# The last chunk of a fused Mamba and expert layer: tiles of 4 states by 256 tokens, and a back half per 256 tokens

## The reference

```python
x = x + attn(layernorm(x))           # attn: y of the scan below, then residual + out inside
x = x + ffn(layernorm(x))            # 8 experts, each for 512 tokens in a row
# attn(x): xn = rmsnorm(x, rms_w); xs, res = split(xn @ W_in)       (512 + 512 channels)
xs = silu(causal_conv4(xs) + conv_b)
dt, Bm, Cm = split(xs @ W_x, [512, 528]); dt = softplus(dt @ W_dt)
A = -exp(A_log)                                                     # 512 channels x 16 states
h = exp(A * dt_t) * h + dt_t * B_t * xs_t                           # per token, channel, state
y_t = sum over states of h * C_t
out = residual + (y * silu(res)) @ W_out
# ffn(x), per expert e: silu(x @ w1[e]) * (x @ w3[e]) @ w2[e]       (256 -> 704 -> 256)
```

## Time and profile before

| what | us |
|---|---|
| median of three runs | 988.26 |
| profiled execution, span of its core | 989.0 |
| PE, DVE, ACT, POOL busy in that span | 922.8, 900.1, 731.6, 891.3 |
| 512 scans, L657 | 623.5 |
| 255 products by C on POOL, L515 | 598.8 |
| 109 and 145 BU products, POOL L501 and DVE L642 | 257.9 and 173.1 |
| 512 exps, L786 | 347.0 |

### The profile page before, as it was taken

The page is one execution under the profiler, slowest core; times in us unless marked ns, Lnnn a source line. Parts: engine busy times, 40 slices in busy tenths (PEclk is TensorE's granted clock), DMA queues, the critical chain, the costliest instruction groups (busy, mean ns, idle before and its releaser), DMA issues.

```text
span 989.0 us, 13017 instructions
## 1 busy us (share of the span) xinstructions
PE 922.8 (93%) x4172; PEld 601.7 (61%) x4172; DVE 900.1 (91%) x966; ACT 731.6 (74%) x1305; POOL 891.3 (90%) x424
## 2 busy tenths in 40 slices
PE   6998998999999999999999999999999998769898
PEld 4555455655866566755756557655767556755765
DVE  5789899899999999999999999999999989999951
ACT  4566877888779877888788887888788786567530
POOL 0388899999999999999999999999999999999920
PEclk9898999999999999999999999999999999679899
DMA  5490136011651038111571037210580127200110
GB/s 174 173 343 22 43 134 252 1 67 59 247 209 45 23 115 351 49 67 43 195 276 43 25 102 299 114 67 0 187 327 3 44 75 290 107 22 1 61 50 21
DMA packets 43476, 116.82 MB, mean 118 GB/s; under 512 B 8592, under 2 KB 27024, under 8 KB 34192
## 3 DMA queue, kind: packets, MB, share of 16 engines
q1 hardware_dynamic: 41552, 115.94, 31.5%
q10 hardware_dynamic: 1856, 0.04, 0.1%
HBM read 110.21 MB, written 5.77 MB: 117 GB/s over the span
## 4 chain that ended last, share of the span: by engine, by line
PE 37%; DVE 36%; ACT 15%; issue 11%; DMA 1%; DVEq 0%; SPq 0%; ACTq 0%
DVE ring L657 25%; PE gbank L1090 19%; DVE ring L642 9%; PE ybank L1153 7%; PE gbank L1104 7%; ACT ebank L786 4%; ACT hb L1019 2%; ACT sres L867 1%; ACT xs L863 1%; PE gbank L1098 1%; ACT L1015 1%; ACT L875 1%; ACT L871 1%; DMA hb<-in_L_attn_W_x_dram 1%; PE gbank L1224 1%
## 5 line engine op out<-in xcount | busy, mean ns | idle before, releaser
L657 DVE TENSOR_TENSOR_SCAN ring<-ebank,state,ring 128x512 f32<-128x512 f32 x512 | 623.5, 1266 | 32.7 <-ACT ebank L786 25.7
L515 POOL TENSOR_TENSOR hc<-ring,c_all 128x1024 f32<-128x1024 f32 x255 | 598.8, 2364 | 17.4 <-DVE ring L657 9.6
L786 ACT ACTIVATE ebank<-dt_,a_neg 128x512 f32<-128x512 f32 x512 | 347.0, 689 | 163.2 <-DVE ring L657 160.6
L1153 PEld LDWEIGHTS ybank<-ident,hc 128*128 128x128 f32 x2048 | 240.2, 145 | 102.9 <-issue 53.1
L1153 PE MATMUL ybank<-ident,hc 128*128 128x128 f32 x2048 | 267.7, 280 | 28.3 <-POOL hc L515 19.6
L501 POOL TENSOR_TENSOR ring<-b_all,u 128x1024 f32<-128x1024 f32 x109 | 257.9, 2366 | 10.5 <-DVE taken L606 9.5
L642 DVE TENSOR_TENSOR ring<-b_all,ubank 128x1024 f32<-128x1024 f32 x145 | 173.1, 1194 | 0.0
L1090 PE MATMUL gbank<-xT,w 128*128 128x512 f32 x320 | 148.9, 599 | 14.7 <-DVE hb L737 11.9
L1090 PE MATMUL gbank<-xT,w_a 128*128 128x512 f32 x256 | 120.2, 606 | 8.0 <-DVE dt_ L631 4.4
L1090 PEld LDWEIGHTS gbank<-xT,w 128*128 128x128 f32 x320 | 57.7, 191 | 82.1 <-issue 57.1
L1090 PE MATMUL gbank<-xs,w_a 128*128 128x512 f32 x224 | 100.8, 593 | 0.7 <-ACT sres L804 0.7
(11 more groups left out here) (145 smaller groups left out, 777.1 us busy)
## 6 DMA issues: line engine op xcount, KB each, us to landing
b_all<-bc_kept SPq DMA_DIRECT2D x32, 1024.0 KB, 6.6
c_all<-bc_kept SPq DMA_DIRECT2D x32, 1024.0 KB, 8.4
w<-in_L_ffn_w_dram SPq DMA_DIRECT2D x16, 640.0 KB, 4.8
w_a<-in_L_attn_W_in_dram SPq DMA_DIRECT2D x7, 1024.0 KB, 4.9
w_a<-wc_kept SPq DMA_DIRECT2D x7, 1024.0 KB, 4.8
w2s<-in_L_ffn_w_dram SPq DMA_DIRECT2D x8, 640.0 KB, 9.3
xin<-in_L_attn_x_dram SPq DMA_DIRECT2D x9, 512.0 KB, 3.5
x<-in_L_attn_x_dram SPq DMA_DIRECT2D x7, 512.0 KB, 6.4
```

What stands on the lines that cost most here:

```text
L515: ch_ok.by(e.tensor_tensor(hc[:, q % HC, :, :], ring[:, q % RING, :, :], c_all[:, n:n + NG, :], ALU.mult))
L657: h_ok.by(e.tensor_tensor_scan(row, ebank[j % 2][:, :], row, initial=state[:, q, n:n + 1], op0=ALU.mult, op1=ALU.add))
L786: e_ok.by(e.activation(ebank[j % 2][:, :], dt_[:, d, :], ACT.Exp, scale=a_neg[:, d, k:k + 1]))
L1153: last = e.matmul(ybank[:, cols(b)], hc[:, q % HC, n, cols(b)], ident[:, :], is_transpose=True, start=(k == 0 and n == 0 and b == 0), stop ...
```

## The change

In chunk 7 the tiles of blocks d = 2 and 3 hold SN = 4 states of HF = 256 tokens. Tiles 16 to 23 are the first 256 tokens (d 2 in 16 to 19, d 3 in 20 to 23), tiles 24 to 31 the second 256. So there are 64 scans and 64 exps of 256 for 32 and 32 of 512. The number of tiles, of products by C and of their elements stays. POOL has 15 BU tiles in this chunk for 14. `u_half` copies both blocks' u for one half of the tokens to ubank. PE's lag is 2 tiles from tile 24 on.

The back half of chunk 6 has its own table in iteration 7, `FINAL`, most of it some four tiles earlier (SiLU after tile 16 for 20, contractions at 20 and 21 for 24 and 28). The first 256 tokens of chunk 7 then go through gating, projection, statistics, normalising, turning, and gate and up products of 256 columns (two results to a bank, "GT" and "UH") beside tiles 22 to 31; SiLU, products and the contractions of blocks 0 and 1 follow after the last exp. The second 256 tokens go through the same after the last scan, with the contractions of blocks 0 and 1 between their steps. The dummy matmuls are gone. Tables for iterations 0 to 6 are the same. The diff, cut:

```diff
+    POOL_BU_E = (1, 4, 7, 8, 11, 14, 16, 17, 18, 19, 21, 23, 25, 26, 29)
+    QH = Q // 2
+    HF = TC // 2
+    SN = 2 * NG
+    LAG_E = 2
+    SWITCH = 24
...
+        FINAL = [
+            (3, "back", "YT", 3, 4.4), (4, "back", "M", 0, 8.9), (4, "back", "M", 1, 8.7), (10, "back", "OXT", 0, 10.9),
+            (11, "back", "GATE", 0, 13.2), (12, "scan", "YT", 0, 12.9), (12, "back", "GATE", 1, 13.4), (13, "back", "GATE", 2, 14.2),
+            (13, "back", "GATE", 3, 14.4), (14, "back", "GATE", 4, 15.2), (14, "back", "TAIL", 0, 16.9), (14, "back", "UP", 0, 16.3),
+            (16, "back", "UP", 1, 16.5), (17, "back", "UP", 2, 17.3), (17, "back", "UP", 3, 18.3), (18, "back", "UP", 4, 19.3),
+            (19, "back", "DOWN", 0, 22.9), (20, "scan", "YT", 1, 20.8), (20, "back", "DOWN", 1, 23.9), (21, "ahead", "M", 0, 28.9),
+            (23, "ahead", "YH", 0, 24.2), (25, "ahead", "YH", 1, 26.2), (26, "ahead", "M", 1, 40.0), (27, "ahead", "OXH", 0, 28.6),
+            (28, "ahead", "GT", 0, 29.5), (28, "ahead", "GT", 1, 29.7), (29, "ahead", "GT", 2, 30.7), (30, "ahead", "UH", 0, 31.5),
+            (30, "ahead", "YH", 2, 31.2), (31, "ahead", "UH", 1, 34.0)]
         LAST = [
...
+            (0, "back", "UH", 2, 3.2), (2, "back", "YH", 3, 2.9), (4, "back", "DN", 0, 9.0), (6, "back", "OXH", 1, 7.0),
+            (7, "back", "DN", 1, 9.2), (8, "back", "GT", 5, 9.6), (8, "back", "UH", 5, 9.8), (9, "back", "GT", 3, 10.2),
+            (10, "back", "UH", 3, 11.0), (11, "back", "GT", 4, 11.5), (12, "back", "UH", 4, 12.8), (13, "back", "DN", 2, 14.0),
+            (14, "back", "DN", 3, 15.0)]
...
+        def halved(c, q):
+            return c == E - 1 and q >= QH
+
+        def spot(c, q):
+            if halved(c, q):
+                m = q - QH
+                return ND // 2 + m // (N // SN) % 2, m % (N // SN) * SN, SN, slice(m // GPD * HF, (m // GPD + 1) * HF)
+            return q // GPD, q % GPD * NG, NG, slice(0, TC)
...
@@ vector, group
-                for n in range(NG):
-                    j = q * NG + n
+                for n in range(many):
+                    j = scans(c, q) + n
                     e_ok.wait(e, c, j + 1)
...
+                    h_ok.by(e.tensor_tensor_scan(row, e_of(c, j), row, initial=all_states[:, first:first + 1],
@@ vector, jobs of iterations 7 and 8
+            def ahead_hidden(c, i):
+                e.wait_ge(s_si, 2)
+                wait_read(e, i, "GT", 2)
+                tail = hb[FR:P, FT, 0:HF]
+                e.tensor_tensor(tail, tail, staged_tail, ALU.mult).then_inc(s_hd, 1)
+                wait_read(e, i, "UH", 0)
+                e.tensor_tensor(hb[:, 0:2, 0:HF], hb[:, 0:2, 0:HF], staged, ALU.mult).then_inc(s_hd, 1)
+                up_half(i, 1, 2, 2, 0)
...
+            final = [(4, "back", gated(ND - 1)), (7, "back", m_stats), (8, "back", scaled2), (12, "scan", gated(0)), (16, "back", hidden(0)),
+                     (16, "back", hidden(1)), (16, "back", hidden_tail), (17, "back", hidden(2)), (18, "back", hidden(3)),
+                     (19, "back", hidden(4)), (20, "scan", gated(1)), (23, "ahead", gated_half(0)), (25, "ahead", gated_half(1)),
+                     (26, "ahead", stats_half(0)), (30, "ahead", gated_half(2))]
+            last = [(1, "back", last_c), (1, "back", ahead_hidden), (1, "back", gated_half(3)), (2, "back", lambda c, i: up_half(i, 2, 4, 1, 0)),
+                    (2, "back", stats_half(1)), (6, "back", normal_last), (6, "back", turned_last), (7, "back", finish)]
@@ scalar, group
-                for n in range(NG):
-                    j = q * NG + n
+                for n in range(many):
+                    j = scans(c, q) + n
                     h_ok.wait(e, c, j - 1)
-                    e_ok.by(e.activation(ebank[j % 2][:, :], dt_[:, d, :], ACT.Exp, scale=a_neg[:, d, k:k + 1]))
+                    e_ok.by(e.activation(e_of(c, j), dt_[:, d, tok], ACT.Exp, scale=a_neg[:, d, n0 + n:n0 + n + 1]))
@@ scalar, jobs
+            def ahead_silus(c, i):
+                e.preload_act_table(ACT.Silu)
+                wait_read(e, i, "GT", 2)
+                e.activation(hb[:, 0:FT, 0:HF], hb[:, 0:FT, 0:HF], ACT.Silu).then_inc(s_si, 1)
+                e.activation(hb[FR:P, FT, 0:HF], hb[FR:P, FT, 0:HF], ACT.Silu).then_inc(s_si, 1)
...
+            final = [(2, "back", y_read(ND - 1)), (4, "back", residual(0, 1)), (8, "back", rooted2), (8, "back", m_copy), (9, "back", normal2),
+                     (10, "scan", y_read(0)), (10, "back", turned("OXT")), (13, "back", gate(0, 1)), (14, "back", gate(2, 3)),
+                     (15, "back", gate(4)), (15, "back", tails), (16, "back", gate_silus), (18, "scan", y_read(1)), (19, "back", down_on(0)),
+                     (20, "back", down_on(1)), (21, "ahead", residual(0)), (22, "back", down_out(0)), (22, "ahead", y_half(0)),
+                     (23, "back", down_out(1)), (25, "ahead", y_half(1)), (26, "ahead", residual(1)), (27, "ahead", ahead_normal),
+                     (28, "ahead", ahead_turned), (29, "ahead", ahead_gates(0, 1)), (29, "ahead", y_half(2)),
+                     (30, "ahead", ahead_gate_tail), (31, "ahead", ahead_up)]
+            last = [(0, "back", ahead_silus), (1, "back", y_half(3)), (3, "back", scales_last), (5, "back", silus_last)]
@@ tensor, jobs of iterations 7 and 8
-            last = [(2, "back", y_last), (5, "back", project_last), (5, "back", keep_clock), (5, "back", turn_last)]
...
+            final += [(20, "back", contract_on(0)), (22, "back", contract_on(1)), (22, "ahead", project_part(0, 0, 1)),
+                      (24, "ahead", project_part(0, 2)), (25, "ahead", project_part(0, 3)), (27, "ahead", project_part(1, 0, 1)),
+                      (31, "ahead", project_part(1, 2))]
```

More of the change, by code:

```diff
@@ L333, in run @@
                         group(i, q)
-                    for at, part, job in (table0 if i == 0 else last if i == E else table):
+                    for at, part, job in (table0 if i == 0 else last if i == E else final if i == E - 1 else table):
                         if at == q and on[part][0]:
@@ L794, in group, with u_half @@
                     u_bank(c + 1, 0)
+            def u_half(c, h):
+                u_ok.wait(e, c, ND)
+                bud_ok.wait(e, c, before(dve_bu(c), QH + h * GPD))
+                ub_ok.by(e.activation(ubank[:, :].rearrange("p (d t) -> p d t", d=ND // 2), u[:, ND // 2:ND, h * HF:(h + 1) * HF], ACT.Copy))
             def u_bank(c, d):
```

438 lines of the change are left out of this document (274 added, 164 removed).

## The result

| kernel | median us (range, runs) | ratio to before, 95% interval |
|---|---|---|
| before, timed beside it | 987.79 (987.21 to 991.09, 4) | |
| after | 994.45 (993.17 to 996.62, 4) | 1.0067 [1.0052, 1.0083] |
| after, timed again | 990.12 (988.38 to 994.94, 10) | 1.0017 [0.9994, 1.0039] |

The first timing makes the kernel 0.7% slower; the interval of the second includes no difference. The forecast was 984.5 us, and neither timing comes near it. Single executions of one kernel spread over some 4 to 8 us: in the profiles the first scan of the last chunk starts anywhere from 834.0 to 838.7 us, in kernels whose chunks 0 to 6 are the same code.

What follows compares the result with a forecast made beforehand. Scans were taken as paced by POOL with DVE just behind, the tail by PE. Scans 5.9 - 1.2 + 1.6 + 2.4 + 0.8 = +9.5, tail -13.3, sum -3.8 from 988.3: 984.5 us; 8 in 10 within 978.5 to 991.

Steps and rivals of the forecast that it cites:

- Tail: After T, the last scan's end: half-size gates and a contraction in the statistics wait end it at T+27.4, -13.3 us.
- rival 3: PE's queue is late at T, the last scan's end; the tail shrinks by 10 only, 987.8 us; chance 0.15.
- Scans, short form: Tiles 16 to 31 of the last chunk: four scans of 256 take 2.74 us per tile for 2.37, +5.9.
- The exp loop: Tiles 16 to 31: two banks make a loop over two short scans of 1.46 us, so DVE waits 0.18 per tile.
- Other work on DVE: Last chunk: one BU product fewer, -1.2 us; gatings, statistics and a tiny product together +1.6.
- Stalls: Last chunk: DVE waits at the SiLU block +2.4 us and beside ACT's other jobs +0.8; bounds -1 and +12.
- costed at nothing: Last chunk: state copies and the first half's PE work, 13 us, taken to fit in PE's 17.6 us idle.
- SiLU block: After tile 16's exps: table load and SiLU make DVE wait 3.7 us for 1.3 before, +2.4.
- Rival 1 (POOL): Last chunk's scans: POOL remains the bound, the last scan ends 2.3 to 5 us later, 977 to 980 us; chance 0.18.
- Rival 2: Tiles 16 to 31: ACT's jobs delay exps with nothing buffered; 12 us of stalls, last scan 18 later, 993 us; chance 0.12.
- Rival 4: Tail starts at PE's lower clock level; each us of work there costs one more, 4 us gives 988.5; chance 0.07.
- 1 us worse: Tail: if POOL were still at work beside DVE's two staged SBUF products, the sum would be about 1 us worse.

Runs made afterwards that it cites:

- the second profile: The changed kernel, unchanged, profiled once more: 125.11 us from chunk 7's first scan to the last scan's end, tail 27.5 us; timed again at 990.12 us.
- Paired banks: Each exp bank holds two 256-token exps: on the kernel before with short scans 990.77 us (1.0027), on the changed kernel 988.09 us (1.0003).
- the exchange of BU products: Tile 17's BU product given to DVE, tile 20's to POOL; in the run that also added dummy matmuls at tiles 2 to 4, 986.17 us.
- the best schedule tried here: Changed kernel with two exps per bank, PE's turn first, dummy matmuls also at tiles 2 to 4, tiles 17 and 20's BU products exchanged: 986.17 us (0.9970).

## Why the prediction was wrong, point by point

**Tail: right.** Predicted T + 27.4, measured 27.5; -13.3 against -13.2. PE's last gates began 12.3 us after T for 12.25. The contraction in the place of the dummy matmuls and the half-size gates did what the sum said, and rival 3's price in the tail did not come.

**Scans, short form: too dear.** Predicted 2.74 us per tile, +5.9. Measured 2.60 (950.38 to 952.98) against 2.37: +3.7. A short scan was recorded at 0.733 (0.72 predicted) and the starts lie 0.65 apart. The exp loop was put at 1.46; in after the first scan of tile 29 (950.38) ends at 951.13, the next exp runs from 951.16 to 951.64, and the third scan starts at 951.69. That is a loop of 1.31, just the time of two scans, so it doesn't show. The 0.14 from exp to scan holds where DVE stands idle for the exp (0.13 in the five such waits of after), but not here, where DVE is still busy. The Trainium skill's rule (VectorE: DVE Perf Modes, section on the TRN2 errata) of a fixed cost per instruction holds in kind: 0.65 is 0.06 more than half of 1.18. For the added scans without the exp loop the rows had given 3.2, the page's figure for operands in SBUF, which the prediction took, an estimated 1.9. One operand of the scan lies in PSUM, for which the same table has 120 cycles: an estimated 4.0. 3.7 was measured.

**Other work on DVE: right but for one instruction.** -1.2 for the BU product, and about +1.5 for the rest where 1.6 stood. But the tiny scale product (L732, 128x4) took 1.41 us for the 0.16 it takes elsewhere: +1.25, and +4.6 in the second profile (see the last section).

**Stalls: the step that failed.** Predicted +3.2 over those of before, measured 14.7 - 2.95 = +11.8 (second profile +9.1). Sum: 3.7 - 1.2 + 1.5 + 1.25 + 11.8 = 17.05 for 9.5. (Second: 3.7 - 1.2 + 1.5 + 4.6 + 9.1 = 17.7, measured 17.6.) What I costed at nothing was PE's work moved forward by four tiles, from the fact that PE was idle for 17.6 us in the window. The same row had its clock at 0.73, and no term stood for work that meets the lower level: the first contraction, moved to 913 us, ran at half speed. And idle time in a window isn't idle time ahead of the instruction that someone waits for. The places:
- *SiLU block.* Predicted a wait of 3.7, measured 3.14 + 0.53: right. Paired banks on the kernel before cut it from 3.1 + 0.5 to 0.5 + 0.9, on after only to 1.9 + 0.9. That DVE has little beside the block there is my reading; the exchange of BU products, which gives it something, went with 0.8 + 0.9.
- *Turn behind the contraction, 3.84 (3.06).* Not in the sum, though the prediction held the mechanism ready ("if that cover fails, the sums of y wait behind it in PE's queue") and then looked for it in the tail. About 1 us is the order; the other 2 to 3 are the lower clock of the contraction.
- *Statistics, 2.24 (0.65).* Not in the sum. They were moved from tile 8 to tile 7, onto a projection that the lower clock stretched from 3.62 to 6.75 us (5.16).
- *Exps behind jobs of ACT that wait for PE, 2.07 at tile 30.* I priced ACT's jobs by their durations, the half microsecond each, and not by what they themselves wait for. In-order ACT hands a wait for PE on to the exps, to DVE and to POOL.

**The rivals.** Rival 1 (POOL) is out: 12.6 us idle. Rival 2, to which I gave 0.12, has the right size (T + 18, 993 us; measured T + 17.05, with a profiled time of 994.4) and half of the right mechanism: the halved buffer of exps costs 5.4 us on the schedule of before, some 3 on that of after, where PE's queue is late too. Rival 3's mechanism was there, in the scans and not in the tail. Rival 4, to which I gave 0.07, had the clock, with its price of one us more for each at the lower level, but in the tail, which ran at 1.00. It was at work in the scans: 2.83 us between two profiles of one program, 2 to 3 in the turn's wait, up to 2.2 in the statistics.

What stays open: how much of the whole the clock makes. Holding it up with dummy matmuls in four tiles left the median where it was, but they delay other work too. More of them took away the wait for the statistics, and the scale product took that time. With its waits gone, this change would need 124.5 - 14.7 = 109.8 us for the scans and would gain some 11 us (an estimate); the best schedule tried here got 5 us of these 14.7 back. That a schedule exists which gets the rest isn't shown.

## What to carry to other kernels

When tiles are cut in half, keep the depth of the buffers in tokens, not in their number: two banks of half size let one long job of the producer through to the consumer (5.4 of 7.7 us here). When a block of work is moved to another place in an in-order queue, write down for each instruction behind it who waits for it and when; the idle share of that engine says nothing on this. Look at the granted clock of the place too: a contraction moved to where PE had been partly idle (3.9 us busy of the 7 up to 910 us) ran at half speed, and the wait behind it grew by the whole difference where one program was seen at both levels (2.83 us for 2.83). Before an experiment is read, look whether its profile and the one beside it had the same clock there: the edit that moved the projection seemed to cost 2.8 us at a place that it doesn't touch. And a gain in a tail is safe to count, since nothing follows it, while the same work laid beside a loop that three engines share has to be paid with slack that each of the three must have at that moment.

## What the runs showed of the hardware

DVE's products of two SBUF operands don't slow down beside POOL in these traces: they end when an instruction of POOL ends. The timeline of after around the small product:

```profile
869.41 2.35 POOL L552 TENSOR_TENSOR hc<-ring,c_all 128x1024 f32<-128x1024 f32 x1 [0.48 <-DVE ring L700]
870.37 1.41 DVE L732 TENSOR_TENSOR st<-st 128x4 f32<-128x4 f32 x1
```

Four columns took 1.41 us; it ends at 871.78, POOL's product at 871.76. In the trace of before the product L691 of the earlier trace rows (1.31 us, from 946.23) ended 0.55 after a POOL instruction ended at 946.99, about the time of 512 columns (0.69 alone, less the 0.15 that the prediction estimated as fixed). The Trainium skill (SBUF — State Buffer, section on its two separate sides) says that the pair of ports shared by the two engines is an exclusive lock and the loser is blocked for the whole instruction. This trace agrees, but in four other profiles the block lasted longer than one instruction. In the second profile of after the small product starts at 866.24. POOL's products followed each other without a pause and ended at 866.39, 868.70 and 871.00, and it ended with the third, at 871.01. POOL's next product then waited 2.46 us for a scan that stands behind the small one. The other three (4.72, 4.76 and 5.32 us) look the same. So my "1 us worse" for a 128x512 product should have been "up to 5 us, even for four columns". What decides between 1.4 and 5 us isn't shown.

Other prices that no row of before had: a scan of 256 lasts 0.733 us and starts 0.65 after the one before it; an exp of 256 takes 0.48; a scan for whose exp DVE stands idle starts 0.13 us after that exp has ended. Contraction instructions take 0.226 us each at the full clock (24 in 5.42) and up to 0.455 at the lower level (12 in 5.46).
